# Attention with seven steps instead of six between a step's scores and its products with the values

## The reference

```python
x = x + layernorm(attention(layernorm(x), ...))     # 4 heads of 64
x = x + layernorm(ffn(layernorm(x), ...))           # 8 experts, one chosen per token

# attention, per batch and head
sim  = einsum('bhid,bhjd->bhij', rmsnorm(q) * 64**-0.5, rmsnorm(k))
attn = softmax(sim, axis=-1)
out  = einsum('bhij,bhjd->bhid', attn, v)           # then @ w_o.T + b_o
```

## Time and profile before

| what | value |
|---|---|
| median of 3 runs | 711.79 us (711.3 to 713.42) |
| the profiled execution | 712.63 us, span of the core 710.9 us |
| busy share of the span: TensorE, VectorE, ScalarE | 87%, 82%, 75% |
| granted TensorE clock, mean | 0.961 of full speed |
| attention of the first and the second batch, from the span's start | some 95 to 294 us, 400 to 592 us |

### The profile page before, as it was taken

The page is one execution under the profiler, slowest core; times in us unless marked ns, Lnnn a source line. Parts: engine busy times, 40 slices in busy tenths (PEclk is TensorE's granted clock), DMA queues, the critical chain, the costliest instruction groups (busy, mean ns, idle before and its releaser), DMA issues.

```text
span 710.9 us, 21562 instructions
## 1 busy us (share of the span) xinstructions
PE 615.4 (87%) x8705; PEld 432.0 (61%) x8717; DVE 584.9 (82%) x1153; ACT 533.6 (75%) x870; POOL 262.0 (37%) x425
## 2 busy tenths in 40 slices
PE   4799788999989999878799799999999998558773
PEld 2677545666656666755576366666666667436662
DVE  4899959988898899898999589888888898967653
ACT  3389788888887888775798788788878887445552
POOL 3134443343334333001577423233233320445554
PEclk9599999999999999999999899999999999979996
DMA  5931188798978988311032688889888873119111
GB/s 169 291 101 41 31 153 157 139 177 167 170 145 161 175 160 164 92 60 59 31 89 77 139 158 153 156 157 163 153 158 158 162 139 121 54 68 310 66 57 46
DMA packets 60665, 92.88 MB, mean 131 GB/s; under 512 B 7057, under 2 KB 29844, under 8 KB 60566
## 3 DMA queue, kind: packets, MB, share of 16 engines
q0 software_dynamic: 35088, 66.13, 48.7%
q1 hardware_dynamic: 24902, 25.37, 12.3%
q10 hardware_dynamic: 576, 0.00, 0.0%
HBM read 15.87 MB, written 14.66 MB: 43 GB/s over the span
## 4 chain that ended last, share of the span: by engine, by line
PE 47%; DVE 25%; DMA 9%; issue 7%; ACT 7%; another core or an unknown queue 2%; POOL 2%; SPq 0%; POOLq 0%; DVEq 0%; ACTq 0%
PE banks L1524 16%; PE banks L1567 7%; PE banks L1566 6%; PE banks L1568 6%; DMA e_h<-e_f 6%; DVE e_l L1102 5%; PE banks L1344 5%; PE banks L1396 3%; DMA e_x<-x_all 2%; DVE x_all L1175 2%; ACT e_f L665 1%; DVE st L1188 1%; DVE e_l L962 1%; DVE e_l L971 1%
## 5 line engine op out<-in xcount | busy, mean ns | idle before, releaser
L665 ACT ACTIVATE e_f<-banks,nbias,c_ 128x1024 f32<-128x1024 f32 x172 | 200.4, 1201 | 55.8 <-PE banks L1524 49.1
L1102 DVE TENSOR_TENSOR e_l<-e_f,e_h 128x1024 f16<-128x1024 f32 x172 | 206.9, 1226 | 37.4 <-DMA e_h<-e_f 29.0
L1524 PE MATMUL banks<-q_T,k_T 128*128 128x512 f16 (+1 forms) x1024 | 215.3, 384 | 7.1 <-DVE e_l L962 3.9
L1568 PE MATMUL banks<-v_mm,e_l 128*128 128x65 f16 x2048 | 205.4, 191 | 0.0
L1568 PEld LDWEIGHTS banks<-v_mm,e_l 128*128 128x128 f16 x2048 | 189.8, 99 | 0.0
L467 POOL DMA_DIRECT2D e_h<-e_f x148 | 78.9, 533 | 190.4 <-PE banks L1568 141.8
L1566 PE MATMUL banks<-v_mm,e_h 128*128 128x65 f16 x1376 | 139.9, 192 | 4.5 <-DVE e_l L1102 2.5
L1566 PEld LDWEIGHTS banks<-v_mm,e_h 128*128 128x128 f16 x1376 | 127.6, 96 | 25.4 <-DVE e_l L1102 9.9
L1567 PE MATMUL banks<-v_mm,e_h 128*128 128x64 f16 x1376 | 140.1, 195 | 0.0
L1567 PEld LDWEIGHTS banks<-v_mm,e_h 128*128 128x128 f16 x1376 | 127.4, 97 | 11.8
L1102 DVE TENSOR_TENSOR e_l<-x_all,e_x 128x1024 f16<-128x1024 f32 x84 | 102.5, 1233 | 13.6 <-DMA e_x<-x_all 10.2
(11 more groups left out here) (296 smaller groups left out, 1189.0 us busy)
## 6 DMA issues: line engine op xcount, KB each, us to landing
e_h<-e_f POOLq DMA_DIRECT2D x148, 256.0 KB, 3.8
e_x<-x_all POOLq DMA_DIRECT2D x72, 256.0 KB, 4.3
x_all<-x SPq DMA_DIRECT2D x12, 512.0 KB, 4.1
rows_d<-e_x SPq DMA_DIRECT2D x1, 5180.0 KB, 24.3
k_T<-k_T SPq DMA_DIRECT2D x16, 256.0 KB, 3.6
k_T<-rows_d SPq DMA_DIRECT2D x15, 259.0 KB, 5.3
q_T<-rows_d SPq DMA_DIRECT2D x5, 259.0 KB, 7.3
x_all<-weT SPq DMA_DIRECT2D x2, 512.0 KB, 10.6
```

Of the source, the lines that this page charges most:

```text
L665: act.activation(whole[s % ALL % NEF], ps_S[s % ALL % 3], ACT.Exp, bias=bias_of(h, k // NT), scale=CESC).then_inc(s_E, 1)
L1102: dve.tensor_tensor(low[s % ALL % NLO], whole[s % ALL % NEF], high[s % ALL % NHI], ALU.subtract).then_inc(s_El, 1)
L1524: return pe.matmul(ps_S[s % ALL % 3][:, c * BANK:(c + 1) * BANK], k_T[rows, 1 - c if cross else c, h * N + j * P:h * N + (j + 1) * P], q_T ...
L1568: ins = pe.matmul(o, low[s % ALL % NLO][:, at], v[:, 0:DH + 1], start=False, stop=j == NT - 1, skip_group_check=True)
```

## The change

`LAG` becomes 7, a new constant `FIRST = 6` keeps the steps at which the loop of rounds begins, and `NHI` becomes 7, so that there is a seventh buffer for the rounded exponentials. `NEF` (6 whole buffers), `NLO` (4 low buffers), the 3 pairs of score banks and the rounds of the scores stay.

```diff
-    LAG = 6
+    FIRST = 6
+    LAG = 7
     OUT = 2
-    NEF, NHI, NLO = 6, 6, 4
+    NEF, NHI, NLO = 6, 7, 4
...
-        e_x = sb("e_x", [P, 2, QB], f16)
+        e_x = sb("e_x", [P, NHI - 4, QB], f16)
...
-        high = [e_h[:, i, :] for i in range(4)] + [e_x[:, i, :] for i in range(2)]
+        high = [e_h[:, i, :] for i in range(4)] + [e_x[:, i, :] for i in range(NHI - 4)]
...
-                open_cross(b * ALL + LAG)
-                open_cross(b * ALL + LAG + 1)
-                for k in range(LAG, ALL - 2, 3):
+                open_cross(b * ALL + FIRST)
+                open_cross(b * ALL + FIRST + 1)
+                for k in range(FIRST, ALL - 2, 3):
                     three_steps(k)
                 last_two_steps()
```

## The result

The changed kernel took 706.61 us in the median of 4 runs (705.27 to 707.04), the kernel before 712.34 us in 4 runs (711.3 to 713.42). The ratio is 0.9917, with a 95% interval from 0.9893 to 0.9941: 5.9 us less, 4.2 to 7.6. The forecast was 707.2 us, 4.6 us less.

What follows compares the result with a forecast made beforehand. TensorE was taken as the bound, with only its standstill to save. Gains of 5.4 and 1.4 us less losses of 1.0 and 1.2 us made 4.6 us: 711.8 to 707.2 us, range 703.5 to 713 us.

Steps and rivals of the forecast that it cites:

- The bound and what can be gained: Attention: TensorE bounds at 4.36 us per round; only its standstill, 10.0 us in six units of both batches, can be regained.
- Late roundings ahead of unit ends: Unit ends: rounding DMAs of about 5.9 us, against a 3.9 us median, delay VectorE's move out; TensorE waits up to 1.25 us.
- One more step covers them: Exponentials to products: one more step gives 1.45 us, more than each mid-attention wait of at most 1.25 us.
- The term of the first batch: First batch: two thirds of 7.2 us plus 0.85 us regained, 5.4 us; bounds 2 and 8 us.
- The term of the second batch: Second batch: two seen waits, 0.47 and 0.37 us, and one like them regained, about 1.4 us; bounds 0.5 and 2.8.
- A seventh high buffer, price nothing: Rounding's target: a buffer added with the distance keeps its release at the same place against the scores, at no cost.
- New waits at first-position ends: Units ending in a round's first product: scores wait 0.2 to 0.3 us through whole and low buffers, 1.0 us in all.
- Waits for ScalarE's rounding: Units ending in a round's second product: score waits of 0.47 us behind ScalarE's own rounding should go.
- Filling: Start of each batch: TensorE has one product less beside the scores, losing 0.6 us per batch, 1.2 us in all.
- Nothing moves: Rival, chance 0.27: ScalarE's waits for subtractions through six whole buffers set the pace; little is regained, 711.5 us.
- The slower rival: Chance 0.10: whole and low buffers bind at the subtraction behind each move out, 0.5 us at 14 ends; 716 us.
- The Trainium skill's rule: Rounding DMA: 2.0 us plus bytes over 436 GB/s, 2.6 us for 256 KB; no subtraction late, so 713.0 us.

Runs made afterwards that it cites:

- the pair with half-size DMAs: Rounding DMAs cut to half the size in the kernel before, distance six (0.9870), and in the changed kernel, distance seven (0.9884).

## Why the prediction was right, point by point

**The bound and what can be gained.** Right in kind: the granted clock (0.961 before, 0.958 after, mean of the span) and TensorE's work did not change. The size of a round was 0.02 us short. In the second batch of the changed kernel 32 rounds take 140.66 us, less 0.5 us of waits at first-position ends, which is 4.38 us each, not 4.36; 0.6 us per batch of what I counted as regainable never was.

**Late roundings ahead of unit ends.** Shown by the half-size DMAs as far as landings go: with shorter ones the waits for the move out nearly go at distance six, 0.5 us instead of 4.4. That it is the late ones among them rests on the rows of before.

**One more step covers them.** The waits for the move out went from 4.4 us to none in the first batch. But one step more did not do this by itself: with six high buffers it is a loss, and the seventh buffer without it takes most of these waits away too, down to 0.9 us. The term of the first batch was 5.4 us, measured 4.6 us in the six units and about 0.4 us to the next move out; with the 0.5 us of new waits taken out of the six units it is 5.4 us. The term of the second batch was 1.4 us; with the 0.5 us of new waits taken out it is 2.1 us. TensorE's timeline of before has four waits in that stretch, of which the sum took two and guessed one more: 0.47 us at 453.23 us, 0.35 us for a move out at 454.19 us, 0.37 us at 501.59 us and 0.47 us at 524.79 us, 1.66 us. The first and the third are in the earlier trace rows; the other two:

```profile
454.19 0.19 PE L1566 MATMUL banks<-v_mm,e_h 128*128 128x65 f16 x1 [0.35 <-DVE attn_x L1126]
524.79 0.60 PE L1524 MATMUL banks<-q_T,k_T 128*128 128x512 f16 x2 [0.47 <-ACT e_f L665]
```

**A seventh high buffer, price nothing.** The sum needed only that it keeps the roundings at their place, and that held: from the end of the product that frees the buffer to the issue it is 0.55 us in the median of both kernels. But the sentence hid what the buffer is worth. Without it the distance is a loss of 11 us; alone it brings 0.5 to 0.6% of the 0.9% by the ratios, and more by the medians. The two halves of the change do not add: both give a rounding more time before its products, one by an earlier issue, the other by a later use. I never asked what each half would do alone, and would have called the buffer a mere companion of the distance.

**New waits at first-position ends.** Predicted 0.2 to 0.3 us at four places; measured 0.24 us at each, on the path as worked out, and gone with a seventh whole buffer where one was tried, in the second batch.

**Waits for ScalarE's rounding.** Those of 0.47 us are gone, as predicted: behind its start the second batch has no row with a score wait on ScalarE left in TensorE's timeline (the new 0.24 us lie inside longer score blocks).

**Filling.** Predicted 0.6 us per batch, and 0.7 us in each batch of the pair with half-size DMAs. With whole-size DMAs the term is there, but hidden under what one rounding DMA happens to take. From the first product of the batch to the end of the last product of step 15 the first batch takes 0.65 us longer in the first profile of the changed kernel (28.94 against 28.30 us), but the second 0.50 us less (26.60 against 27.10). Issue and subtraction of the rounding of step 2 in the second batch, before, in that profile, and in a second one of the same changed kernel:

```profile
400.80 0.53 POOL L467 DMA_DIRECT2D e_h<-e_f  x1 [2.47 <-ACT e_f L665]
406.48 2.36 DVE L1102 TENSOR_TENSOR e_l<-e_f,e_h 128x1024 f16<-128x1024 f32 x2 [3.27 <-DMA e_h<-e_f]
```

```profile
394.20 0.53 POOL L468 DMA_DIRECT2D e_h<-e_f  x1 [2.06 <-ACT e_f L666]
398.19 1.22 DVE L1103 TENSOR_TENSOR e_l<-e_f,e_h 128x1024 f16<-128x1024 f32 x1 [0.59 <-DMA e_h<-e_f]
```

```profile
395.45 0.53 POOL L468 DMA_DIRECT2D e_h<-e_f  x1 [2.06 <-ACT e_f L666]
401.39 2.36 DVE L1103 TENSOR_TENSOR e_l<-e_f,e_h 128x1024 f16<-128x1024 f32 x2 [3.52 <-DMA e_h<-e_f]
```

It took 5.7, 4.0 and 5.9 us. With the 5.9 us the second batch's start takes 27.73 us, 0.63 us longer than before; with the 4.0 us it is shorter. The first batch's start varies as much, from 27.56 to 29.05 us in four profiles with the same program up to there. So one profile of each kernel cannot measure this term.

**Sum.** 4.6 us forecast, 5.9 us (4.2 to 7.6) measured; the forecast lies in the interval, so the 1.3 us between them are not clear of noise. The terms by the profiles: first batch 5.4 us for 5.4, second batch 2.1 for 1.4, new waits 1.0 for 1.0, filling 1.5 for 1.2 by the half-size pair. That is 5.0 us. That the first batch's term is met so closely is luck: of what could be regained there the sum took two thirds, and no row gave that share.

**Rivals.** "Nothing moves" fell: the whole buffers did not hold TensorE back at distance seven but for the new waits, although ScalarE's waits grew from 6.5 to 9.1 us, which the prediction had named as a sign that they would. The slower rival, low and whole buffers as the bound, fell for this change, but its mechanism shows one step further on: at distance eight its waits are in the rows. How much of the 4.5% they make was not parted from the missing high buffer. The Trainium skill's rule ("DMA: Bandwidth & Descriptors", section "Anatomy of one DMA — SWDGE (gpsimd) path"), by which the estimate for the DMA was 2.6 us, fits neither the rows of before nor those after (3.8 to 4.3 us). In the kernels with half the bytes the landing was 2.4 us, and there distance seven gained nothing, as I had said it would if roundings landed early.

## What to carry to other kernels

A software pipeline has more than one depth: the distance in the consumer's order and the number of buffers at each link. Here more distance without the buffer was a loss. Before raising the distance work out, link by link, which buffer's release moves later against its producer. If a late transfer is the trouble, try first one more buffer on the transfer's target without more distance: here it gave more than half of the gain. When a helper engine takes a share of one kind of work (here one rounding in eight), its copy of the wait stands in its own queue with other work behind it, and has to be costed too.

## What the runs showed of the hardware

The same kernel took 12 us less on some chips, and nearly all of it behind attention. The changed kernel reached the first instruction of the second batch's last move out at 589.85 us on one chip and at 588.94 us on another, but its span ended at 703.2 us on the one and at 690.7 us on the other: 113.4 and 101.8 us for the same stage. From the first move out of the first batch to the first of the second the two took 297.99 and 297.26 us. Why the last stage differs was not looked into.

Halving the bytes of a rounding DMA took its landing from 3.9 to 2.4 us and the queue's share from 84.2% to 48.7%, so a part of the 3.9 us goes with the bytes that it or the DMAs ahead of it in the queue move. The runs do not tell these two apart.
